# Moving the transposes of the softmax probabilities behind the value products in TensorE's slot order

## The reference

```python
n = _layer_norm(x, ln1_g, ln1_b)
x = x + _attention(n, n, a1_wq, a1_wk, a1_wv, a1_wo, a1_bo)
n = _layer_norm(x, ln2_g, ln2_b)
x = x + _attention(n, context, a2_wq, a2_wk, a2_wv, a2_wo, a2_bo)
x = _geglu_ff(_layer_norm(x, ln3_g, ln3_b), ff_w1, ff_b1, ff_w2, ff_b2) + x
...
scores_t = jnp.einsum('bhsd,bhtd->bhst', q, k_t) * attn_scale
probs_t = jax.nn.softmax(scores_t, axis=-1)
text_out = jnp.einsum('bhst,bhtd->bhsd', probs_t, v_t)
...
qsem = jnp.einsum('bhst,bte->bhse', probs_t, text_ehs)
```

## Time and profile before

| | us |
|---|---|
| median of 3 runs | 3806.16 |
| lowest and highest run | 3804.15, 3810.74 |
| span of the profiled execution | 3799.1 |
| TensorE busy in it | 3608.9 (95%) |
| ScalarE busy | 2592.4 (68%) |
| VectorE busy | 2547.7 (67%) |
| GpSimd busy | 1352.4 (36%) |

### The profile page before, as it was taken

The page is one execution under the profiler, slowest core; times in us unless marked ns, Lnnn a source line. Parts: engine busy times, 40 slices in busy tenths (PEclk is TensorE's granted clock), DMA queues, the critical chain, the costliest instruction groups (busy, mean ns, idle before and its releaser), DMA issues.

```text
span 3799.1 us, 88944 instructions
## 1 busy us (share of the span) xinstructions
PE 3608.9 (95%) x29708; PEld 3328.8 (88%) x29708; DVE 2547.7 (67%) x8159; ACT 2592.4 (68%) x8021; POOL 1352.4 (36%) x1658
## 2 busy tenths in 40 slices
PE   6999999999999999999999999999999999999997
PEld 5888989889898898988989899898988989889897
DVE  6667666676766666676676766767667676666766
ACT  6667676766767667676676766767676676766764
POOL 2233343333433334333333433334333343333433
PEclk9999999999999999999999999999999999999998
DMA  6522314223142321413223132231422313232130
GB/s 169 163 64 75 103 44 119 60 85 91 41 122 58 96 77 51 123 47 106 70 60 117 45 112 65 76 103 44 121 57 87 90 41 121 58 96 77 53 93 18
DMA packets 210716, 313.38 MB, mean 82 GB/s; under 512 B 31232, under 2 KB 167520, under 8 KB 210272
## 3 DMA queue, kind: packets, MB, share of 16 engines
q1 hardware_dynamic: 209984, 307.53, 27.6%
q10 hardware_dynamic: 288, 0.16, 0.0%
HBM read 267.97 MB, written 14.42 MB: 74 GB/s over the span
## 4 chain that ended last, share of the span: by engine, by line
PE 60%; DVE 17%; ACT 11%; issue 8%; POOL 4%; DMA 1%; SPq 0%; ACTq 0%; DVEq 0%; POOLq 0%
PE PS L818 8%; PE PT L840 6%; PE PV L854 6%; PE PW L798 5%; PE PG L659 5%; ACT SE L989 4%; PE PG L651 4%; PE PG L634 4%; PE PV L864 3%; DVE sums L1233 3%; PE PG L637 3%; PE PG L635 3%; PE PG L636 3%; POOL SE L1404 3%; PE PG L742 2%
## 5 line engine op out<-in xcount | busy, mean ns | idle before, releaser
L1404 POOL TENSOR_TENSOR SE<-SE,rs 128x512 f32<-128x512 f32 (+1 forms) x640 | 557.6, 871 | 1761.8 <-DVE rs L1238 1761.8
L989 ACT ACTIVATE SE<-PS,mx 128x128 f32<-128x128 f32 (+2 forms) x3840 | 982.6, 346 | 240.7 <-DVE qq L1262 128.5
L975 ACT ACTIVATE PTs<-PT 128x512 f32<-128x512 f32 (+2 forms) x960 | 575.4, 599 | 87.1 <-PE PT L840 67.9
L840 PE MATMUL PT<-ident,SE 128*128 128x128 f32 (+2 forms) x3840 | 582.0, 274 | 36.4 <-POOL SE L1404 34.6
L1233 DVE TENSOR_REDUCE sums<-SE 128x4 f32<-128x512 f32 (+1 forms) x640 | 367.0, 573 | 337.8 <-ACT SE L989 336.9
L1222 DVE TENSOR_REDUCE mx<-PS 128x4 f32<-128x512 f32 (+2 forms) x960 | 504.4, 525 | 72.1 <-PE PS L818 58.7
L840 PEld LDWEIGHTS PT<-ident,SE 128*128 128x128 f32 (+2 forms) x3840 | 465.5, 144 | 64.5 <-POOL SE L1404 49.0
L1396 POOL TENSOR_TENSOR n<-qq,p_half 128x4 f32<-128x4 f32 x320 | 345.3, 1079 | 490.2 <-DVE qq L1262 490.1
L798 PE MATMUL PW<-w_o,OTs 128*128 128x160 f32 x2560 | 415.3, 299 | 1.1 <-ACT OTs L967 1.1
L818 PE MATMUL PS<-qk 128*128 128x256 f32 x1280 | 348.5, 395 | 47.6 <-ACT qk L915 47.6
L912 ACT ACTIVATE qk<-PG 128x256 f32<-128x256 f32 x640 | 252.9, 395 | 190.1 <-PE PG L637 186.5
(11 more groups left out here) (207 smaller groups left out, 7828.5 us busy)
## 6 DMA issues: line engine op xcount, KB each, us to landing
q_slice<-q_split SPq DMA_DIRECT2D x630, 192.0 KB, 2.4
vc_slice<-vc_split SPq DMA_DIRECT2D x155, 512.0 KB, 3.6
kc_slice<-kc_split SPq DMA_DIRECT2D x150, 256.0 KB, 2.7
q1st<-q_hi SPq DMA_DIRECT2D x320, 32.0 KB, 1.9
k1st<-k_hi SPq DMA_DIRECT2D x160, 38.5 KB, 1.9
xres<-in_x_dram SPq DMA_DIRECT2D x32, 160.0 KB, 2.3
q1st<-q_lo SPq DMA_DIRECT2D x160, 32.0 KB, 1.9
out_dram<-x SPq DMA_DIRECT2D x64, 80.0 KB, 1.6
```

The lines of the kernel that those rows point to most:

```text
L840: last = tr(PT[0:J, 128 * i:128 * i + 128], SE[:, place % 4, J * i:J * i + J], ident[:, :])
L975: a_(PTs[0:J, place % 3, :], PT[0:J, :], ACT.Copy).then_inc(S["pts_done"], 1)
L989: last = a_(SE[:, place % 4, J * i:J * i + J], PS[place % 2][:, step * i:step * i + J], ACT.Exp, bias=mx[:, place % 2, i:i + 1])
L1404: gp.tensor_tensor(e, e, rs[:, n % 2, :].unsqueeze(2).to_broadcast([128, 4, J]), ALU.mult)\
```

## The change

In the loop that writes TensorE's instructions, the call of `probs_transposed` is moved from ahead of the value jobs, the output products and the value products of its slot to right behind the value products, still ahead of the late jobs. Nothing else is changed; the instructions of ScalarE, VectorE, GpSimd and SyncE stand in the same order as before.

```diff
--- before.py
+++ after.py
@@ -873,8 +873,6 @@
                         scores(UNIT_AT[t + 1])
                     for name in qk_at(t):
                         job(name)
-                    if t - PT_LAG in UNIT_AT:
-                        probs_transposed(UNIT_AT[t - PT_LAG])
                     for name in late_at(t):
                         if name[0] == "v":
                             job(name)
@@ -883,6 +881,8 @@
                             wo(*u[1:])
                     for u in products_at(t):
                         probs_v(u)
+                    if t - PT_LAG in UNIT_AT:
+                        probs_transposed(UNIT_AT[t - PT_LAG])
```

## The result

| | us |
|---|---|
| after, median of 4 runs | 4007.77 (4006.91 to 4012.48) |
| before, median of 4 runs | 3808.45 (3804.15 to 3812.24) |
| ratio, with its 95% interval | 1.0528 (1.0513 to 1.0543) |
| span of the profiled execution, after and before | 4005.2 and 3799.1 |

The change costs 199 us of the median and 206.1 us of the span. The forecast was 129. The sign and the mechanism are as predicted, the size is not: 4008 lies above the range's end of 3990.

The account below looks back on a forecast made before the run. TensorE, busy 3608.9 of 3799.1 us, bounds the kernel, beside a chain of other engines. Losses of 4.75 and 3.9 less 0.3 won make 8.35 us a period, 125 in 15, plus 4: 129, so 3935 us; range 3845 to 3990.

Parts of the forecast that it names:

- Terms a to g: Seven groups of later waits per full period, in slots 11 to 41 and 51 to 54: 4.75 plus 3.9 us.
- a to d: The firmest four terms, in slots 11 to 27: delays passed on by the late copy, 4.75 us a period together.
- a: Slots 11 to 15: copy 1.34 us later, delaying exponential, VectorE's sums, `qq` and the scores by 1.3 us a period.
- b: Slots 15 to 18: later copy delays, through an exponential that waited for `qq`, the waiting scores by 1.35 us a period.
- the gain of slot 25: Transposes' 1.26 us wait for GpSimd in slot 25: claimed not won, since the wait moves to the value job ahead.
- slots 42 to 50 and 54 to 10: Rest of the period: ScalarE's delayed instructions end 0.3 us or more ahead of whoever waits; cost taken as nothing.
- c: Slots 19 to 22: copy 0.77 us later, through an exponential that waited for `qq`, delays scores by 0.75 us a period.
- first period and tail: Start without l1 units and end with VectorE between: given 4 us together, bounds 0 and 15.
- The rival that the clock falls: Granted clock at 0.89 for a period, TensorE's 223.7 us taking 27 more, in all 15 periods; chance 0.01.
- That the time falls by the gap that is covered: Transposes' waits for GpSimd are covered and the copies hide: at most 34.6 us gained, 3771; chance 0.07.
- That nothing moves: Gains and losses cancel, or the copy's start wasn't bound by the transposes: 3806 us; chance 0.04.
- That only a part of the chain is paid: Losses at one place leave ScalarE a head start at the next: half the sum, 3870 us; chance 0.17.

## Why the prediction was right in its mechanism and short in its size

**Right: what the time turns on.** The copy follows the transposes, the exponential follows the copy, and VectorE and the scores follow the exponential. Both single slots, 11 and 23, gave the terms of the forecast where they were looked for, and leaving out seven slots gave back what their terms say. Terms a to g add to 8.65 us a period in the forecast and to 8.82 in the traces; none is off by more than 0.16. a to d were each about 0.1 short; in a and b that is the copy's start, 0.28 us behind the scores where the forecast took 0.19.

**Right: the gain of slot 25 is not won.** The wait of 1.26 at the transposes became 1.27 at the value job. The gain forecast as 0.3 a period was 0.45, in slot 5.

**The step that failed: "In the rest of the period (slots 42 to 50 and 54 to 10), ScalarE's delayed instructions end 0.3 us or more ahead of whoever waits, ... so I cost these at nothing."** They cost 3.63 us a period, 54 us. Two things were left out in the subtraction. First, ScalarE's queue holds the 1.28 us load of its function table behind the copy (slots 8 and 56, 2.02 us a period). Before, the load was in time for the product by 0.50, so a copy that is late by more than that is paid from there on. Taking the load ahead of the copy gave back 26 us. Second, I followed the delayed instruction to its next reader, and not through VectorE's queue behind that reader: in slot 49 the exponential waits 1.02 for `qq`, the copy of the queries stands behind it, and TensorE waits 0.52. This exponential had waited for `qq` in the kernel before as well, as those of b and c had, and that row was there to be subtracted; it started 0.03 us behind the slot's opening scores and starts 1.81 behind them now. This part (slots 2, 49, 54, 55: 1.61 a period) rests on the timeline and on the run of these slots alone, which has both parts in its 48 us; no run takes this one alone. Here is slot 49's exponential in the kernel before:

```profile
2029.47 0.96 ACT L989 ACTIVATE SE<-PS,mx 128x73 f32<-128x73 f32 x4 [0.65 <-DVE qq L1262]
```

And the rows of slot 49 in the changed kernel:

```profile
2133.44 0.59 ACT L975 ACTIVATE PTs<-PT 77x512 f32<-77x512 f32 x1 [0.75 <-PE PT L840]
...
2135.05 0.96 ACT L989 ACTIVATE SE<-PS,mx 128x73 f32<-128x73 f32 x4 [1.02 <-DVE qq L1262]
...
2136.54 0.77 PE L818 MATMUL PS<-kx,qk 128*128 128x154 f32 x4 [0.52 <-ACT qk L912]
```

**The second term that was too small: first period and tail.** 4 us were forecast, with bounds 0 and 15; they took 11.2 + 12.5 = 23.7. The reasons given (no l1 units in the one, VectorE between in the other) named why a term might be smaller, and no row was subtracted for either. The run with the full periods alone gave back 16.2 of it. What waits there has not been followed row by row; in the tail a part is the clock (last section).

**The third: the clock.** The rival that the clock falls was priced as a whole period at 0.89. What happens is smaller and local: 8.7 us in slot 18 of 6 periods, and a part of the tail.

Together: 52 for the places costed at nothing (3.63 less the 0.15 by which slot 5 gave more than the forecast's 0.3, times 15), 20 for first period and tail, 9 for the clock in slot 18, 3 for a to g, less 5 in the other slots and less 3 for the clock in slot 32 of the kernel before, make 76; missing were 206.1 - 129 = 77.

**The range.** Its upper end, 3990, allowed 58 us more in the uncosted places, which would have held their 52. It fell short because first period, tail and clock were not added to it at their own bounds. (3935 + 58 is 3993, not 3990; the measured 4008 lies outside either.)

**The rivals.** That the time falls by the gap that is covered fell: the transposes wait no more, and the time rose by 199. That nothing moves fell with it. The rule of the Trainium skill (Perfetto Trace Analysis, Optimization Strategy), by which one finds the gaps of the most contended engine and starts sooner what blocks it, names the engine rightly; here the gap was 34.6 us, and the change made what blocked TensorE elsewhere start later. That only a part of the chain is paid fell too: b's full 1.47 stood behind a's, though both lie within seven slots.

**Signs.** The prediction named its own sign of being wrong, waits that grow in slots costed at nothing, and it came: L634's wait for L1164 went from 1.7 to 27.2 us. Right were the copy's wait (918.0), the vanished wait for GpSimd, the new waits of L798 for OTs (40.8), of L864 and L854 for PTs (12.7 and 2.4), of L642 and L659 for their tile (20.9 and 9.5), and the stretch of 9.3 us (9.41). Wrong were three. A period was to last 240.4 us and lasts 244.1 in the mean (3661.1 / 15, before 3478.7 / 15 = 231.9). L818's wait for `qk` was to pass 80 us and reached 57.7 + 11.3 = 69.0, probably since part of it moved to waits ahead of the scores. TensorE's busy sum was to stay and rose from 3608.9 to 3681.4. Counted in the two traces, 183 more matmuls stand right behind an idle time, and such a one adds 0.37 us to the busy sum where another adds 0.12; 154 more ran at the lower clock and add 0.24 each. That makes some 65 of the 72.5 us, an estimate.

## What to carry to other kernels

When work on the busiest engine is put later in its queue, subtract rows for whoever waits for it, and go on along the in-order queue of that engine, all its instructions and table loads included, until a wait is met that has slack. A place costed at nothing needs its own subtraction, as do prologue and tail. And where a queue mixes a copy that waits with independent work that somebody two engines on waits for, put the independent work ahead of the copy: it gave 54 us back here, of which 17 us (0.46%) came in the kernel before too, which had no such loss.

## What the runs showed of the hardware

**TensorE's granted clock falls for a few us inside a busy stretch, in some periods and not in others.** Windows of the changed kernel, in slot 18 and just behind it, then of the kernel before at the same slot, and of the kernel before in slot 32 of another period:

```profile
2009.48:2012.92 3.44, 3.44 (x14) 2.92 (x15) 2.69 (x11) 1.44 (x5) 1.01 (x1) 0.55 0.23 73
2014.14:2016.20 2.06, 2.06 (x16) 1.96 (x15) 0.00 (x0) 1.88 (x6) 0.21 (x1) 1.00 0.26 84
```

```profile
1912.15:1914.04 1.89, 1.89 (x13) 1.79 (x14) 1.82 (x6) 1.44 (x5) 1.01 (x1) 1.00 0.49 138
...
1502.90:1506.30 3.40, 2.98 (x14) 2.98 (x15) 2.87 (x14) 1.84 (x7) 1.40 (x2) 0.50 0.08 24
```

The granted clock is 0.55, about the lower level of 1.2 GHz, for 3.4 us, and the matmuls in it take longer:

```profile
2006.96 1.09 PE L864 MATMUL PV<-gv,PTs 73*128 73x86 f32 x8 [0.51 <-DVE SE L1260]
...
2009.48 1.73 PE L818 MATMUL PS<-qk 128*128 128x256 f32 x4 [0.99 <-ACT qk L915]
```

The four scores take 1.73 instead of 1.10. TensorE had waited 0.51 and 0.99 us shortly before; ahead of the fall in the kernel before it had waited 0.84 and 0.71 (L696 at 1501.39, L634 at 1503.33). Each fall in slot 18 cost 1.35 to 1.6 us, and it came in 6 periods of 15 with the same instructions in all. The full periods of the kernel before have 2 falls, both in slot 32; with slot 11 or slot 23 moved alone there are 7 in slot 32, and 3 or 7 in slot 25; with the transposes behind the value job there are 15 in each of the two; and with seven slots left in the old order there is none. So their number alone moves a kernel's time, by 20 us in the kernel with the transposes behind the value job, and a change of some us has to be read slot by slot. That the short waits bring the falls is an inference from what stands ahead of them. They can't be all of it: both waits of slots 17 and 18 stand in all 15 periods (0.49 to 0.52 and 0.98 to 0.99 us), and no run tests what else it takes. In the tail, where TensorE waits more, the clock was 0.73 against 0.89 in the earlier trace rows:

```profile
3920.00:4005.20 85.20, 69.87 (x403) 62.21 (x403) 50.32 (x214) 32.90 (x104) 28.60 (x33) 0.73 0.04 10
```

**A small gap for nothing that is waited for.** In the changed kernel the transposes' weight loads stand 408 times behind an idle time of 0.17 us each, put down to issue: 69.9 us in all, 1.0 before.

```profile
PEld PT L840 <- issue: 69.9, 408, 0.2
```

Slots whose order changed and where nobody waits longer (0, 1, 3, 4, 9, 23, 28) stayed within 0.07 us of before, so these gaps probably come in the place of others (before, 365 of 0.17 us stood at the value products, 60.8 us), and I count nothing for them.
